# Moving half of the query/key projections and the value products in an attention block on one Trainium2 core

## The chip, the cores and the metric

The kernel runs on one core of a Trainium2 (trn2) chip. The metric is device time in microseconds (us). Before the change three runs took 684.49, 684.83 and 686.05 us, median 684.83.

## The reference

1024 tokens of width 512 go through two blocks. Both start with a layer norm over the 512 features and add their result to the residual stream. The second block is the one that the change touches. Cut to that:

```python
xn = layernorm(x)                                   # (1024, 512)
# attention, in the kernel's case one sequence of 1024 tokens, 32 heads of 16
q, k, v = xn @ Wq.T + bq, xn @ Wk.T + bk, xn @ Wv.T + bv
att = softmax(where(causal, q @ k.T / 4, -inf))     # per head
attn = (att @ v) @ Wo.T + bo
# feed-forward: a linear layer and 8 low-rank experts of rank 16
base = xn @ base_W.T + base_b
p = softmax(xn @ router_W.T + router_b)             # 15 routes, all of them kept
w = sum of p over the routes that map to an expert  # (1024, 8)
lora = ((xn @ A.T) * w) @ B.T * 2
x = x + attn + base + lora
```

The first block (a gated feed-forward of width 1248, a series of six terms and a top-2 low-rank mixture) is left as it is; it takes the first 250 us or so.

## The kernel before

**Arithmetic.** fp32 operands are split into a high and a low fp32r part. A product is then three matmuls, hi by hi, lo by hi and hi by lo (`product`, lines 894 to 896). ACT makes the high part and DVE the low part; for weights these are `split_hi` (line 696) and `split_lo` (line 1207), for projections `project_hi` (802) and `project_lo` (1413).

**Weights.** `weight_items` (line 75) lists 512 KB items in the order of use. SP loads them one after another into the two halves of `stage`, and ACT and DVE split each one to where it is used: two halves of `ring_hi`/`ring_lo`, or a place of its own. Item n is loaded once item n-2 is split. `ring_done` (468) says which projection frees a ring half.

**Queries and keys.** Each of the four 128-column parts m of the query and key projections serves two groups of four heads, groups 2m and 2m+1. A part is made by `project` (1004), 24 matmuls of 128x512 into one of two PSUM slots of two banks. ACT and DVE split it into `nat`, one set of SBUF tiles (a tile for q, one for k, each with a high and a low half), and SP stores both halves to `heads_dram` (`store`, 548). `project_hi` of part m waits until part m-1 has been stored (806), since all parts use the same tiles. `stack(g)` (523) loads group g from `heads_dram` in eight transfers, laid out so that a head's two query halves and one key half, with rows of ones, are the contraction rows. Four sets of stack tiles are used in turn: three of their own, and the last is what xt_hi and xt_lo leave free.

**Order on PE in the stage before attention.** After the first block's last transposes: q0 and the router, k0, q1, k1, q2, k2, q3, k3 (1035 to 1038), the rank-16 projection `a`, the gate transposes, eight value tiles (`values`, 1080) and eight tiles of the linear layer (`linear`, 1091). Between these stand the units of `maxima` (1048), 20 a group, which make a group's scores once to take each row's maximum; DVE reduces them in `row_max` (1451). Values carry the units of group 0, the linear layer those of group 1, and the attention steps those of groups 2 to 7, two groups ahead (`max_plan`, 228). `turn_maxima` (1074) transposes a group's finished maxima, `negate_max` (1467) negates them, `neg_max` (556) writes them into the query stack. The linear tiles end with the low-rank product from `hw1`, which lies in the ring half of item qk3 (466). `psum_users` (266) is the written-out order of everything that uses the two PSUM slots; the users take them alternately, and each waits for the one two places before it.

**Attention.** Eight groups of twelve steps (`QSTEPS`, 169). A step is a key tile against up to 512 queries of one half: widths 512, 384, 256, 128 in the first half, then 512, 384, 512, 256, 512, 128, 512, 512. Each step has four scores (`score`, 1123), one a head, in the order of heads 0, 2, 1, 3. At 512 or 384 columns each has a bank of its own, out of three used in turn. At 256 or 128 columns two heads share a bank (`score_bank`, 216): the first and third score fill one, the second and fourth the other, and ACT is told of a bank only when it is full. A score that opens a bank waits for the exponential of three banks before it. ACT takes the exponentials (872), POOL masks diagonal tiles (690), and `weigh_values` (1143) multiplies the probabilities of the step two before (LAG = 2) by the values into `bank[3]`: eight matmul records of 32 columns. `extras` (255) adds maxima units after the second and the fourth score, and in groups 6 and 7 parts of the output projection, three matmuls each, after the fourth. The value products stand last in a step (1183). Twice a group `take_u` (810) has ACT copy `bank[3]` out, ahead of the exponentials of steps 2 and 6, and the first value product of the next half waits for it (1151).

Issue order is the program's on every engine; PE, ACT, DVE, POOL and SP run on their own and wait on semaphores.

```python
1182                        k = STEPS * g + s - LAG
1183                        if hh == GH - 1 and k >= 0:
1184                            weigh_values(k)
```

Of the kernel before, what the change touches and what calls it, by code (L numbers as in the profile page):

```python
# [24 lines left out]
F32 = mybir.dt.float32  # L25
# [47 lines left out]
def weight_items():  # L73
# [192 lines left out]
def psum_users():  # L266
# [23 lines left out]
def build(nc, stream, router1, x_in, vec, bias_rows, discount, expert_map, heads_dram, den_dram, out):  # L290
    nodes = ExitStack()
    with nodes:
# [68 lines left out]
        u_sb = sb(block1, "u_sb", [P, 2, HALF])  # L361
        den = sb(block1, "den", [P, 2, DEN_COLS])
# [92 lines left out]
        for n, (dest, name) in enumerate(ITEMS):  # L455
            item_at[(name, sum(1 for d, m in ITEMS[:n] if m == name))] = n
            if dest == "ring":
                ring_at[n] = len(ring_at)
# [7 lines left out]
        hw1 = ring_of(f"qk{KD - 1}")[1:]  # L466
# [28 lines left out]
        def res(name):  # L495
# [6 lines left out]
        nat = {("q", 0): attn_hi[:, 2, :], ("q", 1): attn_lo[:, 2, :],  # L502
               ("k", 0): attn_hi[:, 3, :], ("k", 1): attn_lo[:, 3, :]}
# [4 lines left out]
        def _(sp):  # L508
# [11 lines left out]
            for n in range(2, item_at[("qk3", 0)] + 1):  # L520
                weights(n)

            def stack(g):
# [4 lines left out]
                if g < STACKS - 1:  # L528
                    sp.wait_ge(S["blank"], g + 1)
                if g == STACKS - 1:  # L530
                    sp.wait_ge(S["y_done"], NT)
# [16 lines left out]
            def store(which, m):  # L548

                sp.wait_ge(S[f"{which}_free"], m + 1)  # L550
                for part in range(2):
                    first = heads_dram[m, "qk".index(which), 0, part * HD]
                    sp.dma_start(bass.AP(first.tensor, first.offset, [[2 * HD * TOK, 2 * GH], [TOK, HD], [1, TOK]]),
                                 nat[which, part].bitcast(F32)).then_inc(S[f"{which}_stored"], 16)
# [61 lines left out]
            for g in range(GROUPS):  # L616
# [23 lines left out]
        def _(pool):  # L640
# [32 lines left out]
            for g in range(STACKS - 1):  # L673
# [4 lines left out]
            for t in range(NT):  # L678
                pool.tensor_tensor(x_sb[:, t, :], x_sb[:, t, :], bo_bc, ALU.add).then_inc(S["y_biased"], 1)
# [15 lines left out]
        def _(act):  # L695
            def split_hi(n):
# [6 lines left out]
                if dest == "base0":  # L703
                    act.wait_ge(S["q_stored"], 32 * KD)
                    act.wait_ge(S["k_stored"], 32 * KD)
                if dest == "wo0":
                    act.wait_ge(S["y_done"], NT)
# [92 lines left out]
            turned_hi(7)  # L800

            def project_hi(which, m):
# [4 lines left out]
                act.activation(nat[which, 0], slot_of((which, m))[:].rearrange("p a n -> p (a n)"), ACT.Identity,  # L807
# [10 lines left out]
            def attn_split_hi(m, half):  # L818
                k = 2 * m + half
                act.wait_ge(S["attn_f"], k + 1)  # L820
                if k == 0:
                    act.wait_ge(S["y_done"], NT)
                at = slice(half * HALF, (half + 1) * HALF)
# [7 lines left out]
            for m, names in enumerate((["qk2"], ["qk3"], ["lora1", "wv0"]), 1):  # L831
                for name in names:
                    split_hi(item_at[(name, 0)])
                project_hi("q", m)
                project_hi("k", m)
            split_hi(item_at[("wv1", 0)])
            act.wait_ge(S["a_ready"], 1)
            act.activation(lora_h1, slot_of(("a", 0))[:].rearrange("p a n -> p (a n)"), ACT.Copy
                           ).then_inc(S["a_free"], 1)
            act.wait_ge(S["w_free"], 1)  # L840
# [745 lines left out]
```

## Time and profile before

| what | us |
|---|---|
| median of three runs | 684.83 (684.49 to 686.05) |
| the profiled execution | 683.69 |
| its span, first to last instruction | 681.9 |
| PE busy in it | 613.8 (90%) |
| DVE / ACT / POOL busy | 377.8 / 293.3 / 77.0 |
| mean granted TensorE clock | 0.956 of full |

The profiled execution took 1.8 us more than its span, and 1.1 us less than the median. Times in rows are counted from the span's start. A row of the timeline gives start, duration, engine, line, operation, the tiles written and read, the shape, how many instructions it merges, and in square brackets the idle time of the engine ahead of it with what ended that. A matmul's duration contains its way through the array, so rows overlap: the time that PE needs for one is the distance between starts. A granted clock of 1.00 is 2.4 GHz, 0.50 is 1.2 GHz. The stages are: first block to 250 us, its tail and projections to 336, values to 373, linear layer to 416, attention to 662, tail to the end.

### The profile page before, as it was taken

The numbers are of one execution on the slowest core, as the hardware profiler recorded it, in microseconds if no ns is written. First come the engines' busy times: TensorE is split into PE (matmuls) and PEld (weight loads), VectorE is DVE, ScalarE is ACT, GpSimd is POOL, SyncE is SP. The second block draws the span as 40 slices with busy tenths as digits, with TensorE's granted clock in tenths as the row PEclk, the third lists the DMA queues.
The fourth block names the chain that finished last, engine by engine and source line by source line (L and its number), as shares of the span: only waits on it lengthen the run. The fifth ranks groups of instructions, "written<-read, shape, count | busy, mean of one in ns | idle before, by whom it ended". The sixth has DMA issues, their size and how long they took to land.

```text
span 681.9 us, 9359 instructions
## 1 busy us (share of the span) xinstructions
PE 613.8 (90%) x3688; PEld 404.4 (59%) x3688; DVE 377.8 (55%) x555; ACT 293.3 (43%) x509; POOL 77.0 (11%) x106
## 2 busy tenths in 40 slices
PE   2999999999999997974798987999999999998993
PEld 2788888878888874763566665434444444444441
DVE  5676553266543354622367457478898798822025
ACT  3456342133422222211321114577777677775540
POOL 3000000000000018100000222121211212121100
PEclk9999999999999997998799997599999899999996
DMA  6313313101111020469751001441633610100003
GB/s 218 123 63 124 122 64 124 62 32 62 43 52 62 32 79 15 125 206 178 266 181 32 3 1 31 75 95 36 111 75 65 108 30 18 26 20 17 21 18 135
DMA packets 24304, 53.64 MB, mean 79 GB/s; under 512 B 8880, under 2 KB 9392, under 8 KB 24256
## 3 DMA queue, kind: packets, MB, share of 16 engines
q1 hardware_dynamic: 23844, 52.33, 28.2%
q0 software_dynamic: 288, 0.58, 0.4%
q8 instruction: 29, 0.48, 0.3%
q10 hardware_dynamic: 128, 0.13, 0.1%
q14 instruction: 15, 0.12, 0.1%
HBM read 39.77 MB, written 10.61 MB: 74 GB/s over the span
## 4 chain that ended last, share of the span: by engine, by line
PE 75%; DVE 9%; DMA 7%; ACT 6%; issue 2%; SPq 1%; ACTq 0%; DVEq 0%
PE bank L1155 11%; PE bank L1138 10%; PE slot L894 8%; PE bank L894 7%; PE slot L896 7%; PE slot L895 7%; PE bank L896 7%; PE bank L895 7%; DMA heads_dram<-attn_lo 6%; PE slot L1061 5%; ACT probs L872 4%; PE slot L1069 2%; DVE maxcol L1460 2%; DMA stage<-in_stream 1%; PE slot L910 1%
## 5 line engine op out<-in xcount | busy, mean ns | idle before, releaser
L872 ACT ACTIVATE probs<-bank 128x512 f32<-128x512 f32 (+2 forms) x320 | 155.6, 560 | 71.4 <-PE bank L1138 69.6
L1460 DVE TENSOR_REDUCE maxcol<-slot 128x2 f32<-128x1024 f32 (+2 forms) x112 | 125.0, 1142 | 44.8 <-PE slot L1069 23.4
L894 PE MATMUL slot<-xt_hi,ring_hi 128*128 128x512 f32 (+2 forms) x248 | 99.7, 402 | 22.1 <-DVE attn_lo L1416 18.6
L895 PE MATMUL slot<-xt_lo,ring_hi 128*128 128x512 f32 (+2 forms) x248 | 98.4, 397 | 0.0
L896 PE MATMUL slot<-xt_hi,ring_lo 128*128 128x512 f32 (+2 forms) x248 | 98.2, 396 | 0.0
L1138 PE MATMUL bank<-qst,kst 50*128 50x512 f32 (+3 forms) x288 | 79.9, 444 | 6.8 <-ACT probs L872 5.9
L1155 PE MATMUL bank<-probs,v_sb 128*32 128x512 f32 (+3 forms) x768 | 85.4, 519 | 0.1
L1138 PEld LDWEIGHTS bank<-qst,kst 50*128 50x128 f32 x288 | 36.8, 199 | 68.2 <-ACT probs L872 59.4
L894 PEld LDWEIGHTS slot<-xt_hi,ring_hi 128*128 128x128 f32 (+2 forms) x248 | 47.4, 191 | 35.2 <-issue 22.0
L1061 PE MATMUL slot<-kst,qst 48*128 48x512 f32 (+3 forms) x288 | 58.3, 397 | 7.7 <-DVE maxcol L1460 7.6
L690 POOL TENSOR_SCALAR_AFFINE_SELECT probs<-probs 128x512 f32<-128x512 f32 x64 | 41.8, 653 | 200.9 <-ACT probs L872 200.9
L1460 DVE TENSOR_REDUCE maxrest<-slot 128x2 f32<-128x768 f32 (+3 forms) x48 | 49.7, 1044 | 21.3 <-PE slot L1069 21.1
L895 PEld LDWEIGHTS slot<-xt_lo,ring_hi 128*128 128x128 f32 (+2 forms) x248 | 47.6, 192 | 10.4
L896 PEld LDWEIGHTS slot<-xt_hi,ring_lo 128*128 128x128 f32 (+2 forms) x248 | 47.2, 190 | 10.7
L1371 DVE TENSOR_TENSOR h_f<-slot,silu 128x512 f32<-128x512 f32 (+1 forms) x20 | 13.8, 691 | 70.3 <-ACT silu L771 70.3
L771 ACT ACTIVATE silu<-slot 128x512 f32<-128x512 f32 (+1 forms) x20 | 12.0, 598 | 90.1 <-PE slot L896 90.0
L1061 PEld LDWEIGHTS slot<-kst,qst 48*128 48x128 f32 x288 | 31.2, 199 | 18.9 <-DVE maxcol L1460 11.5
L1069 PE MATMUL slot<-late_key,late_row 64*128 64x128 bf16 x512 | 35.8, 229 | 0.0
L1210 DVE TENSOR_TENSOR ring_lo<-stage,ring_hi 128x1024 fp32r<-128x1024 f32 x27 | 32.9, 1219 | 3.8 <-ACT ring_hi L708 3.8
L807 ACT ACTIVATE attn_hi<-slot,vec_sb 128x1024 fp32r<-128x1024 f32 x8 | 8.9, 1116 | 54.2 <-DMA heads_dram<-attn_lo 41.5
L1416 DVE SCALAR_TENSOR_TENSOR attn_lo<-slot,vec_sb,attn_hi 128x1024 fp32r<-128x1024 f32 x8 | 10.3, 1283 | 39.6 <-ACT attn_hi L807 39.6
L894 PE MATMUL bank<-res_hi,h_hi 128*128 128x512 f32 (+1 forms) x80 | 32.0, 400 | 0.2
(186 smaller groups left out, 880.8 us busy)
## 6 DMA issues: line engine op xcount, KB each, us to landing
stage<-in_stream SPq DMA_DIRECT2D x43, 512.0 KB, 3.5
heads_dram<-attn_hi SPq DMA_DIRECT2D x8, 512.0 KB
heads_dram<-attn_lo SPq DMA_DIRECT2D x8, 512.0 KB
qst<-heads_dram SPq DMA_DIRECT2D x12, 256.0 KB, 5.7
kst<-heads_dram SPq DMA_DIRECT2D x12, 256.0 KB, 9.7
stage<-u_sb SPq DMA_DIRECT2D x64, 32.0 KB, 2.0
out_y<-x_sb SPq DMA_DIRECT2D x8, 256.0 KB, 2.2
stage<-den_dram SPq DMA_DIRECT2D x15, 128.0 KB
```

Of the source, the lines that this page charges most:

```text
L690: pool.affine_select(out=part, in_=part, compare_op=ALU.is_ge, fill=0.0, base=0, pattern=[[0, GH], [1, P]], channel_multiplier=-1).then_in ...
L872: act.activation(probs[:, to:to + heads, 0:n], bank[b % 3][:, 0:heads * n].rearrange("p (h n) -> p h n", n=n), ACT.Exp, scale=HD ** -0.5). ...
L894: pe.matmul(out_ap, a[0], b[0], start=start, stop=False)
L895: pe.matmul(out_ap, a[0], b[1], start=False, stop=False)
L896: return pe.matmul(out_ap, a[1], b[0], start=False, stop=stop)
L1061: last = pe.matmul(ps[:, side, k * n:(k + 1) * n], queries(g)[rows, sl, i * P:(i + 1) * P], keys(g)[rows, sl, c:c + n], start=(k == 0), st ...
L1069: last = pe.matmul(ps[:, side, (k + 1) * n - P:(k + 1) * n], late_row[rows, part, :], late_key[rows, part, :], start=False, stop=(part == ...
L1138: last = pe.matmul(bank[b % 3][:, at * n:(at + 1) * n], keys(g)[rows, hh % 2, j * P:(j + 1) * P], queries(g)[rows, hh % 2, q0:q0 + n], sta ...
L1155: last = pe.matmul(bank[3][32 * hh:32 * hh + 2 * HD, c0:HALF], v_sb[:, j, (GH * g + hh) // 2, HD * (hh % 2):HD * (hh % 2 + 2)], probs[:, ( ...
L1210: dve.tensor_tensor(lo, stage[:, n % 2, :], hi.bitcast(F32), ALU.subtract).then_inc(S["w_lo"], 1)
L1371: dve.tensor_tensor(h_f[0:m, :], ps[0:m, 1, :], silu[0:m, :], ALU.mult).then_inc(S["h_f_ready"], 1)
L1460: dve.tensor_reduce(per_head[:, :, slots[0]:slots[-1] + 1], scores, AX.X, ALU.max).then_inc(S["max_free"], 1)
```

## The change

It does four things.

1. **Half of the projections go elsewhere.** Only q0, k0, q1 and k1 stand before `a`. q2 and k2 come between the values and the linear layer, q3 and k3 between the linear layer and attention, each pair with a `turn_maxima` between its two. The list of weights, SP's order, ACT's and DVE's orders and `psum_users` follow: the value weights are loaded and split before the projections, base0 and base1 are split after tiles 3 and 5 (ACT) and 4 and 6 (DVE) of the values, and SP loads stack 0 as soon as k0 is stored.
2. **Two sets of tiles.** `natural(which, m, part)` replaces `nat`: odd parts use the old tiles, even parts the third stack's tiles. `project_hi` of part m waits for the store of part m-2. Stack 2 gets its rows of ones by a transfer instead of a memset.
3. **`hw1` has tiles of its own**, 8 KB of each partition; the space reserved for POOL's transfer descriptors goes from 8192 to 2048 bytes of each partition. POOL adds the bias to residual tile t once value tile t is done.
4. **The value products move** from behind a step's fourth score to behind its second, and the extras of that place.

```diff
-    for m in range(KD):
-        add("ring", f"qk{m}")
-    add("ring", "lora1")
+    add("ring", "qk0")
+    add("ring", "qk1")
     for n in range(2):
         add(f"v{n}", f"wv{n}")
+    add("ring", "lora1")
+    add("ring", "qk2")
     for n in range(2):
         add(f"base{n}", f"base{n}")
+    add("ring", "qk3")
...
-    users += [("r", 0)] + [(which, m) for m in range(KD) for which in ("q", "k")]
+    users += [("r", 0)] + [(which, m) for m in range(2) for which in ("q", "k")]
     users += [("a", 0), ("w", 0)]
     for g in range(2):
-        users += [("max", UNITS * g + u) for u in range(UNITS)] + [("m", g)]
+        users += [("max", UNITS * g + u) for u in range(UNITS)] + [("q", 2 + g), ("m", g), ("k", 2 + g)]
...
+        hw1 = [sb(block1, f"hw1_{n}", [P, TOK], F32R) for n in ("hi", "lo")]
...
-        nat = {("q", 0): attn_hi[:, 2, :], ("q", 1): attn_lo[:, 2, :],
-               ("k", 0): attn_hi[:, 3, :], ("k", 1): attn_lo[:, 3, :]}
+        def natural(which, m, part):
+            if m % 2:
+                return (attn_hi, attn_lo)[part][:, 2 + "qk".index(which), :]
+            return (qst, kst)["qk".index(which)][:, 2, part, :]
...
-            for m, name in enumerate(("lora1", "wv0", "wv1", "base0")):
-                store("q", m)
-                store("k", m)
-                weights(item_at[(name, 0)])
-                if m in (1, 2):
-                    stack(m - 1)
+            store("q", 0)
+            store("k", 0)
+            stack(0)
+            store("q", 1)
+            weights(item_at[("base0", 0)])
+            store("k", 1)
             weights(item_at[("base1", 0)])
+            stack(1)
+            weights(item_at[("qk3", 0)])
+            weights(item_at[("wo0", 0)])
+            store("q", 2)
+            neg_max(0)
+            store("k", 2)
             stack(2)
-            for name in ("wo0", "wo1"):
-                weights(item_at[(name, 0)])
-            neg_max(0)
+            weights(item_at[("wo1", 0)])
+            store("q", 3)
             neg_max(1)
+            store("k", 3)
...
             for t in range(NT):
+                pool.wait_ge(S["v_done"], t + 1)
                 pool.tensor_tensor(x_sb[:, t, :], x_sb[:, t, :], bo_bc, ALU.add).then_inc(S["y_biased"], 1)
...
                 act.wait_ge(S[f"{which}_ready"], m + 1)
-                if m >= 1:
-                    act.wait_ge(S[f"{which}_stored"], 32 * m)
-                act.activation(nat[which, 0], ...
+                if m >= 2:
+                    act.wait_ge(S[f"{which}_stored"], 32 * (m - 1))
+                if m == 3:
+                    act.wait_ge(S["y_done"], NT)
+                act.activation(natural(which, m, 0), ...
...
-            project("k", 0)
-            for m in range(1, KD):
-                project("q", m)
-                project("k", m)
+            for m, which in ((0, "k"), (1, "q"), (1, "k")):
+                project(which, m)
...
             for t in range(NT):
                 values(t)
+            project("q", 2)
+            turn_maxima(0)
+            project("k", 2)
...
             for t in range(NT):
                 linear(t)
+            project("q", 3)
             turn_maxima(1)
+            project("k", 3)
...
-                        if hh == GH - 1 and k >= 0:
+                        if hh == 1 and k >= 0:
                             weigh_values(k)
...
+            project_lo("k", 0)
             for t in range(NT):
                 prod = hw_f1[:, t * NE * ROUTES:(t + 1) * NE * ROUTES].rearrange(
...
-                   dynamic_dma_scratch_size=8192)
+                   dynamic_dma_scratch_size=2048)
```

## Rows read from the trace of the kernel before

**Rows 1.** Waits, whole span: engine, line, what for; us, times, longest.

```profile
PE slot L894 <- DVE attn_lo L1416: 18.6, 5, 12.8
```

**Rows 2.** Timeline of PE, projections: first matmuls after waits, one projection, a slow restart.

```profile
296.42 0.47 PE L894 MATMUL slot<-xt_hi,ring_hi 128*128 128x512 f32 x1 [2.98 <-DVE attn_lo L1416]
...
302.71 0.47 PE L894 MATMUL slot<-xt_hi,ring_hi 128*128 128x512 f32 x1 [0.57 <-DVE attn_lo L1416]
...
308.01 0.39 PE L896 MATMUL slot<-xt_hi,ring_lo 128*128 128x512 f32 x1
...
328.56 0.76 PE L894 MATMUL slot<-xt_hi,ring_hi 128*128 128x512 f32 x1 [12.84 <-DVE attn_lo L1416]
...
332.11 0.46 PE L896 MATMUL slot<-xt_hi,ring_lo 128*128 128x512 f32 x1
```

**Rows 3.** Timeline of ACT and DVE: how a projection is split.

```profile
270.05 1.11 ACT L807 ACTIVATE attn_hi<-slot,vec_sb 128x1024 fp32r<-128x1024 f32 x1 [9.68 <-PE slot L896]
...
271.20 1.28 DVE L1416 SCALAR_TENSOR_TENSOR attn_lo<-slot,vec_sb,attn_hi 128x1024 fp32r<-128x1024 f32 x1 [2.77 <-ACT attn_hi L807]
```

**Rows 4.** Queue of SP, ACT's wait for a store, and a stack's transfers with their landing.

```profile
273.30 0.59 SPq L553 DMA_DIRECT2D heads_dram<-attn_lo  x1
...
282.81 1.12 ACT L807 ACTIVATE attn_hi<-slot,vec_sb 128x1024 fp32r<-128x1024 f32 x1 [4.41 <-DMA heads_dram<-attn_lo]
...
451.29 2.37 SPq L543 DMA_DIRECT2D qst<-heads_dram  x4
453.70 1.82 SPq L543 DMA_DIRECT2D kst<-heads_dram  x4
...
kst<-heads_dram SPq DMA_DIRECT2D x2, 256.0 KB, 7.0
```

**Rows 5.** Timeline of PE: the wait ahead of attention, and where group 1 starts.

```profile
418.30 0.39 PE L1077 MATMUL slot<-ident,maxcol 128*32 128x128 f32 x1 [2.06 <-DVE maxcol L1464]
...
451.85 0.50 PE L1138 MATMUL bank<-qst,kst 50*128 50x512 f32 x2
```

**Rows 6.** Windows: busy us of PE, PEld, DVE, ACT, POOL; clock, DMA share, GB/s.

```profile
418.00:442.00 24.00, 23.06 (x143) 12.80 (x147) 12.72 (x15) 14.00 (x28) 3.46 (x6) 0.51 0.41 73
...
534.00:562.00 28.00, 27.28 (x250) 12.53 (x250) 23.20 (x28) 20.63 (x43) 5.54 (x8) 0.94 0.43 78
```

**Rows 7.** Timeline of PE and ACT: a 512-column step of group 3 with maxima.

```profile
506.95 0.50 PE L1138 MATMUL bank<-xt_hi,xt_lo 50*128 50x512 f32 x2
...
507.29 0.35 PE L1061 MATMUL slot<-kst,qst 48*128 48x384 f32 x2
...
507.54 2.06 ACT L872 ACTIVATE probs<-bank 128x512 f32<-128x512 f32 x4 [0.26 <-PE bank L1138]
507.56 0.47 PE L1138 MATMUL bank<-xt_hi,xt_lo 50*128 50x512 f32 x1
...
508.19 0.49 PE L1138 MATMUL bank<-xt_hi,xt_lo 50*128 50x512 f32 x1 [0.16 <-ACT probs L872]
...
508.85 1.06 PE L1155 MATMUL bank<-probs,v_sb 128*32 128x512 f32 x8
...
509.84 0.44 PE L1138 MATMUL bank<-xt_hi,xt_lo 50*128 50x384 f32 x2
```

**Rows 8.** The same engines: step 2 of group 3, two heads a bank.

```profile
512.64 0.50 PE L1138 MATMUL bank<-xt_hi,xt_lo 50*128 50x256 f32 x4
...
512.77 0.60 ACT L816 ACTIVATE u_sb<-bank 128x512 f32<-128x512 f32 x1 [0.76 <-PE bank L1155]
513.27 1.08 ACT L872 ACTIVATE probs<-bank 128x512 f32<-128x512 f32 x2
```

**Rows 9.** Timeline of PE: a 512-column step of group 7 without extras.

```profile
626.24 0.73 PE L1138 MATMUL bank<-xt_hi,xt_lo 50*128 50x512 f32 x3
...
627.48 0.50 PE L1138 MATMUL bank<-xt_hi,xt_lo 50*128 50x512 f32 x1 [0.51 <-ACT probs L872]
...
628.91 0.61 PE L1138 MATMUL bank<-xt_hi,xt_lo 50*128 50x384 f32 x3
```

More of the change, by code:

```diff
@@ L519, in _ @@
             sp.dma_start(x_sb[:, 4:8, :], x_in[4:8].rearrange("t p d -> p t d")).then_inc(S["x_landed3"], 16)
-            for n in range(2, item_at[("qk3", 0)] + 1):
+            for n in range(2, item_at[("qk2", 0)] + 1):
                 weights(n)
@@ L527, in stack @@
                     sp.wait_ge(S["st_ready"], banks_before(g - STACKS + 1, 0))
-                if g < STACKS - 1:
+                if g < 2:
                     sp.wait_ge(S["blank"], g + 1)
+                if g == 2:
+                    for which in "qk":
+                        sp.wait_ge(S[f"{which}_stored"], 32 * 3)
                 if g == STACKS - 1:
-                    sp.wait_ge(S["y_done"], NT)
+                    sp.wait_ge(S["k_ready"], KD)
+                if 2 <= g < STACKS:
                     for side in range(2):
@@ L553, in store @@
                     sp.dma_start(bass.AP(first.tensor, first.offset, [[2 * HD * TOK, 2 * GH], [TOK, HD], [1, TOK]]),
-                                 nat[which, part].bitcast(F32)).then_inc(S[f"{which}_stored"], 16)
+                                 natural(which, m, part).bitcast(F32)).then_inc(S[f"{which}_stored"], 16)
             def neg_max(g):
@@ L672, in _ @@
             pool.wait_ge(S["xn_ready"], 2 * NT)
-            for g in range(STACKS - 1):
+            for g in range(2):
                 pool.memset(keys(g).rearrange("p b n -> p (b n)").bitcast(F32), 1.0).then_inc(S["blank"], 1)
@@ L800, in _ @@
             turned_hi(7)
+            for n in range(2):
+                split_hi(item_at[(f"wv{n}", 0)])
             def project_hi(which, m):
@@ L804, in project_hi @@
                 act.wait_ge(S[f"{which}_ready"], m + 1)
-                if m >= 1:
-                    act.wait_ge(S[f"{which}_stored"], 32 * m)
-                act.activation(nat[which, 0], slot_of((which, m))[:].rearrange("p a n -> p (a n)"), ACT.Identity,
+                if m >= 2:
+                    act.wait_ge(S[f"{which}_stored"], 32 * (m - 1))
+                if m == 3:
+                    act.wait_ge(S["y_done"], NT)
+                act.activation(natural(which, m, 0), slot_of((which, m))[:].rearrange("p a n -> p (a n)"), ACT.Identity,
                                bias=bias).then_inc(S[f"{which}_hi"], 1)
@@ L830, in _ @@
             project_hi("k", 0)
[L831 to L836, printed above, removed]
+            split_hi(item_at[("lora1", 0)])
+            project_hi("q", 1)
+            project_hi("k", 1)
             act.wait_ge(S["a_ready"], 1)
@@ L839, in _ @@
                            ).then_inc(S["a_free"], 1)
+            split_hi(item_at[("qk2", 0)])
             act.wait_ge(S["w_free"], 1)
-            act.wait_ge(S["k_ready"], KD)
-            act.activation(hw1[0], hw_f1, ACT.Copy).then_inc(S["hw_hi_ready"], 1)
+            act.activation(hw1[0][:], hw_f1, ACT.Copy).then_inc(S["hw_hi_ready"], 1)
             act.wait_ge(S["k_ones"], 1)
@@ L848, in _ @@
                                ).then_inc(S["v_free"], 1)
-                if t in (1, 3):
-                    split_hi(item_at[(f"base{t // 2}", 0)])
+                if t in (3, 5):
+                    split_hi(item_at[(f"base{t // 2 - 1}", 0)])
+            project_hi("q", 2)
+            project_hi("k", 2)
+            split_hi(item_at[("qk3", 0)])
             for t in range(NT):
@@ L1407, in _ @@
             turned_lo(7)
+            for n in range(2):
+                split_lo(item_at[(f"wv{n}", 0)])
             dve.wait_ge(S["const_ready"], 9)
@@ L1435, in _ @@
             spread(gate_x1, gate, NT)
-            project_lo("k", 0)
-            for m, names in enumerate((["qk2"], ["qk3"], ["lora1", "wv0"]), 1):
-                for name in names:
-                    split_lo(item_at[(name, 0)])
-                project_lo("q", m)
-                project_lo("k", m)
-            split_lo(item_at[("wv1", 0)])
+            split_lo(item_at[("lora1", 0)])
+            project_lo("q", 1)
+            project_lo("k", 1)
             dve.wait_ge(S["w_ready"], 1)
```

35 lines of the change are left out of this document (22 added, 13 removed).

## Prediction

> **What bounds the kernel.** I read the page first: PE busy 90%, and three quarters of the chain that ended last on PE, so only PE's waits and its clock are to be won or lost. The table of waits, PE alone, gives the stage before attention: PE waited 18.6 us in five places for DVE's low part of a projection, 12.8 in one [rows 1]. Its timeline shows them, and that the last began a restart at half clock: eight starts from 328.56 to 332.11 are 0.44 us apart against 0.23 before [rows 2]. DVE only follows ACT, and ACT waits until the previous part is stored: the second half of q0's store is issued at 273.30, ACT goes on at 282.81, 9.5 us later [rows 4]. So one set of tiles and the stores bound that stage. The next view is the wait ahead of attention, 2.06 us for the last maxima [rows 5], and the windows: from 418 to 442 the clock is 0.51 [rows 6]. Group 0 begins behind the transpose at 418.30, about 418.6, and ends at 451.85: 33.2 us; groups 1 and 2 take from there to 506.95, 27.6 each [rows 5, 7].
> In attention the thing to see is the loop between PE and ACT. A 512-column step starts at 506.95; ACT's first exponential starts 0.59 later; the fourth score waits for it and starts at 508.19; maxima, products at 508.85, next step at 509.84: 2.89 us [rows 7]. Without extras it is 2.67, with 0.51 idle [rows 9].
>
> **Projections apart, two sets.** A projection is 24 starts, 302.71 to 308.01, so 5.5 us [rows 2]. q0's end is marked by ACT's row at 270.05 [rows 3]; k0 starts about 270.6, and k0, q1, k1 and `a` end near 292.8, transposes 293.6, the first value tile (12 matmuls, 2.9) 296.5. None waits for a store: q1 and k1 have other tiles. DVE splits k0 before the gate products now. The waits [rows 1] (18.6) and the slow restart (8 x 0.21 = 1.7) [rows 2] go, and the wait for the last maxima (2.06) [rows 5] lies under q3: 22.4 us out.
> Late next is stack 0, which PE needs at 296.5. k0's split ends about 278.8, its store's second half is issued about 279.6, and with 9.5 it is stored at 289.1; a stack takes from 451.29 to one issue past 453.70 plus 7.0, about 10 us [rows 4]: 299, a wait of 2.5 (0 if nothing queues, 9 if transfers crowd).
> New waits stand where k2 and k3 take the slot that q2 and q3 just filled: `psum_users` leaves one short transpose between. ACT 1.11, DVE 1.28 and handovers are 2.6 [rows 3], less 0.3: 2.3 each. q2 waits some 0.6 for its slot. In: 2.5 + 0.6 + 4.6 = 7.7. Net -14.7.
> Each of the three waits over 2 us may bring half clock. The 2.98 us wait did not, the 2.06 with another ahead did [rows 2, 5]. Ends 0 and 3 x 1.7; I take one, 1.7: **-13.0**.
> The other moves I cost at nothing. The value weights' splits lie in DVE's and ACT's wait for the router. SP passes q1's and k1's stores, base0 and base1 behind stack 0, where nobody needs them for 12 us; stack 1, two ones rows in stack 2 and `neg_max(0)` have 30 us; if that cover went, each costs its 10 us. POOL's bias adds wait for values, read much later. POOL's six transfers keep their time if the smaller descriptor space holds them; if not, the first four wait for each other's landing, up to three landings of 7.0 [rows 4], 21 us at the start; they are few and small, so I leave that end out of the range. The page DMA: Bandwidth & Descriptors of the Trainium skill (SWDGE vs HWDGE) says those descriptors live in reserved SBUF rings; no row shows one full.
>
> **The clock at attention's start.** q3 and k3 are dense, but ACT owes k3's bias pass before the first exponential. Group 0's 33.2 us against 27.6 for the next two [rows 5, 7] bounds it: 0 to -5.6. Nearest is the 2.98 us wait with full clock, but two weight splits of ACT follow, so I take half: **-3**.
>
> **Products after the second score.** A full step now issues a pair of scores (506.95 to 507.29, 0.34), a maxima unit (to 507.56, 0.27), products with their wait (0.1 + 0.99), the second pair (0.34) and a unit with its diagonal (0.6): 2.64 against 2.89 [rows 7]. The wait for the step's first exponential is gone, since the products lie over it. Without extras the loop is 2.67 [rows 9] against 0.34 + 1.09 + 0.34 = 1.8, where ACT's four exponentials (2.06) become the bound.
> Against this stand two costs. (a) Steps of 256 and 128 columns, four of twelve, fill a bank only with the third score. Before, ACT could start after the four scores; now after the products too, up to 0.99 later. Step 7 (256 columns, no unit) shows it: pair 0.2, products about 0.9, pair 0.2, so the bank is full at 1.3, its exponential runs from 1.7 to 2.2, and the second score of step 8, which waits for it, starts at 2.3 where it could at 1.6 before: +0.7. Step 9 does the same to step 10, and step 3 to step 4. While PE multiplies, ACT has used up what was in the banks, so it starts late in the step after as well. (b) Step 2's products wait for `take_u`. Counted from step 1's start: pair 0.3, maxima 0.2, products 1.1, third score at 1.6, ACT from 2.15 with four of 0.41 to 3.8, copy 0.6, products 4.5, third score 5.5, step 2's exponentials from 5.8. Before, they started at 513.27, 3.4 after 509.84 [rows 7, 8]: 2.4 later, of which ACT's slack (0.76 idle before the copy alone [rows 8]) gives some back. Step 6 does this again, milder.
> Laid out so, with these durations, a group of maxima steps changes by: step 0 -0.2, steps 1 to 4 +2.0, 5 and 6 0, 7 to 9 (256, 512, 128) +1.9, 10 and 11 +0.4: +4.1. Groups 1 to 5: +20.5; group 0, whose first steps lack products, +1.9; group 6 -0.4; group 7, without maxima, gains 0.7 a full step against the cost of step 2: -3.5. **+18.5**. Ends: only the idle goes (8 x -0.25 in five groups, -5 in the last two: -15) and every cost in full (+6 a group: +35). I stay near the laid-out value, since it rests on rows 7 and 8.
> PE then idles more, and the clock already dipped in group 4 (0.94 over 28 us, about 1.7 us) [rows 6]. One more dip: **+2** (0 to the rival's).
>
> **Sum.** 683.7 (the profiled execution) - 13.0 - 3 + 18.5 + 2 = 688.2. It lay 1.1 below the median, so I predict 689.3; this case alone reaches 681 to 698. A measurement here tells 0.2%, 1.4 us, from no change.
>
> **Rivals.**
> *The products' move is free or gains.* ACT is idle a quarter of attention, and its late starts in narrow steps could be absorbed there; then only the removed idle counts. For it: the 0.51 us idle per step is in the rows [rows 9]. Against: three banks leave ACT no work while PE multiplies. Attention between -15 and +3, nearest -2: 683.7 + 1.1 - 13 - 3 - 2 = 667 (654 to 673). It decides at an attention cost under 14. Chance 0.23.
> *Half clock inside attention.* More idle per step brings the state of 418 to 442 [rows 6] back, at 5.6 us a group [rows 5]. With four groups: 689.3 + 22 = 711 (698 up). For: group 4's dip. Against: all other groups kept full clock. Chance 0.17. TensorE: Matmul & The Clock Gate of the Trainium skill (A second HAM failure mode) describes short idles between matmul groups, from cycling PSUM banks, as making the clock oscillate; by that rule this rival is the forecast, and group 4's dip agrees.
> *Stack 0 is late.* Stores and stack crowd, as they did when ACT waited longest; 6.5 more: 696. Chance 0.10.
> *The forecast* has 0.50.
>
> **Chances.** Faster: the first rival's 0.23 and 0.08 of the forecast's low end, 0.31. Same: 0.07. Slower: 0.62. The range, 664 to 704, holds the forecast, the third rival, most of the first and the start of the second.
>
> **What would show it.** Right: q1 to `a` without gaps over 0.6; values start near 294 and a PE wait for stack 0 of 1 to 4 us; two PE waits of 2.3 before k2 and k3; attention starting near 404; no wait of the fourth score; groups 1 to 5 of 31 to 33 us, with ACT idle over 1 us before steps 2, 3, 7 and 9, PE waiting at step 2's products for `u_sb`. Wrong: groups of 28 or less, or PE's clock at 0.5 for whole groups.

## The result, and the profile after

The changed kernel takes 707.88 us, median of four runs (700.97, 707.63, 708.12, 725.87), against 685.44 for the kernel before on the same chip: ratio 1.029, interval 1.0211 to 1.0368, so slower. The forecast was 689.3 with a range of 664 to 704: the sign was right, the size was not. Medians are over all runs, while ratios and intervals leave out, on both sides, the runs that are over about 1.5% longer than the fastest of the same kernel, so a ratio is not the quotient of the two medians. The profiled execution is the run of 700.97; its span is 699.2 at a mean clock of 0.954. The two middle runs had 0.937 and 0.942, the longest 0.904. The median is 6.9 us above the profiled execution, at a lower clock, and this trace does not show where that time lies.

In the changed kernel's numbering line 1163 is the scores (1138 before), 1180 the products with the values (1155), 896 the exponentials (872), 1083 the maxima (1061), 918 to 920 the three matmuls of a product (894 to 896), 1443 the low parts of the projections (1416), 835 the copy `take_u` makes of u (816).

The projections first. PE's waits from 280 to 420 (us in total, times, longest), which answer to [rows 1]:

```profile
PE slot L918 <- DVE qst L1443: 2.5, 1, 2.5
PE slot L918 <- DVE attn_lo L1443: 2.5, 1, 2.5
PE slot L918 <- DVE maxrest L1486: 0.6, 1, 0.6
```

and the timeline of PE there, which answers to [rows 2, 5]:

```profile
294.54 0.39 PE L920 MATMUL bank<-attn_hi,xt_lo 128*128 128x512 f32 x1
295.90 0.44 PE L1083 MATMUL slot<-kst,qst 48*128 48x128 f32 x4 [0.97 <-issue]
...
330.27 0.47 PE L918 MATMUL slot<-xt_hi,ring_hi 128*128 128x512 f32 x1 [0.59 <-DVE maxrest L1486]
...
333.94 0.45 PE L918 MATMUL slot<-xt_hi,ring_hi 128*128 128x512 f32 x1
...
340.19 0.47 PE L918 MATMUL slot<-xt_hi,ring_hi 128*128 128x512 f32 x1 [2.51 <-DVE qst L1443]
...
344.37 0.40 PE L920 MATMUL slot<-xt_hi,ring_lo 128*128 128x512 f32 x1
...
397.87 0.47 PE L918 MATMUL slot<-xt_hi,ring_hi 128*128 128x512 f32 x1 [2.50 <-DVE attn_lo L1443]
...
402.23 0.43 PE L918 MATMUL slot<-xt_hi,ring_hi 128*128 128x512 f32 x1
...
405.08 0.49 PE L1163 MATMUL bank<-qst,kst 50*128 50x512 f32 x2
```

The 12.8 us wait and its four companions are gone, the first value tile ends at 294.9, and attention starts at 405.08 instead of about 418.6: 13.5 us are won. What came in: 0.59 before q2, 2.51 before k2, 2.50 before k3, and a stretch at half clock behind each of the three. From 330.27 to 333.94 there are 9 steps from start to start, which at full clock take 2.04 (0.227 each): 1.6 lost. 340.19 to 344.37 loses 1.7 over 11 steps, 397.87 to 402.23 loses 1.6 over 12.

Then attention. The windows are groups 0, 3 and 6, then group 7 up to where the clock falls in the tail (busy us of PE, PEld, DVE, ACT, POOL; clock, DMA share, GB/s).

```profile
405.10:442.85 37.75, 35.07 (x226) 16.32 (x225) 20.00 (x19) 21.76 (x43) 4.46 (x7) 0.64 0.41 84
...
509.80:542.50 32.70, 29.05 (x266) 13.85 (x265) 23.92 (x27) 20.07 (x43) 5.10 (x8) 1.00 0.33 68
...
607.80:644.10 36.30, 33.71 (x203) 15.64 (x199) 11.18 (x17) 22.50 (x46) 5.64 (x9) 0.95 0.07 17
644.10:685.60 41.50, 36.94 (x209) 16.60 (x208) 9.45 (x15) 21.89 (x44) 5.41 (x9) 0.96 0.12 34
```

Here are the starts of the groups in both traces, and under each row of starts the lengths:

```
group              0      1      2      3      4      5      6      7+tail
before, start   418.62 451.85 479.72 506.95 535.14 563.59 591.80 626.24
before, length   33.2   27.9   27.2   28.2   28.5   28.2   34.4   55.7
after, start    405.08 442.85 477.30 509.78 542.54 575.02 607.79 644.10
after, length    37.8   34.5   32.5   32.8   32.5   32.8   36.3   55.1
```

Attention and tail grew from 263.3 to 294.1, by 30.8: +4.5 in group 0, +25.0 in groups 1 to 5, +1.9 in group 6, -0.6 after it. Groups 2 to 5 are at full clock, so their 32.6 against 27.7 (groups 2, 3 and 5 before, two even and odd neighbours averaged) is order, not clock: 4.9 a group. PE is busy 29.05 of 32.7 us where it was busy 27.28 of 28 [rows 6].

The page shows who waits. ACT has the same work as before and 104.5 us of idle ahead of its exponentials instead of 71.4, for scores; PE has a new wait, 4.2 in the row of the products. The first row is of the kernel before, the others of the changed one:

```profile
L872 ACT ACTIVATE probs<-bank 128x512 f32<-128x512 f32 (+2 forms) x320 | 155.6, 560 | 71.4 <-PE bank L1138 69.6
...
L896 ACT ACTIVATE probs<-bank 128x512 f32<-128x512 f32 (+2 forms) x320 | 155.2, 559 | 104.5 <-PE bank L1163 104.3
...
L1180 PE MATMUL bank<-probs,v_sb 128*32 128x512 f32 (+3 forms) x768 | 87.9, 531 | 4.8 <-ACT u_sb L835 4.2
```

**Step by step.** The products of one step follow those of the last, so the distance between their starts is a clean ruler for a step, even where a score's record is missing. Mean of two neighbouring groups at full clock (a group with and one without its `turn_maxima`); the column is the step into which the distance leads, widths 512, 384, 256, 128, 512, 384, 512, 256, 512, 128, 512, 512. E1 (below) has the projections of the changed kernel and the products of the kernel before; its distances are those of before.

```
step     0    1    2    3    4    5    6    7    8    9    10   11   sum
E1      2.26 2.62 1.88 1.36 3.00 2.59 2.30 1.66 2.93 1.36 2.47 3.26 27.7
after   2.42 2.85 2.98 2.39 3.01 2.93 2.34 2.72 3.04 2.43 2.34 3.20 32.6
E6      2.41 2.85 2.98 1.79 2.52 2.93 2.34 2.13 2.50 1.83 2.02 3.20 29.5
E9      2.41 2.85 2.98 1.36 2.38 2.94 3.39 1.66 2.15 1.83 2.02 3.20 29.2
E5      2.42 2.85 2.98 1.36 2.16 2.93 3.39 1.66 1.94 2.54 1.48 3.20 28.9
```

The loss stands in the four steps of 256 and 128 columns (2, 3, 7 and 9), 1.0 to 1.1 each, 4.3 of the 4.9. The full steps, where I had looked for a gain of 0.25 each, have mostly none. Step 7 of group 3 in the changed kernel, PE and then ACT:

```profile
528.43 0.50 PE L1163 MATMUL bank<-xt_hi,xt_lo 50*128 50x512 f32 x2
...
528.99 0.28 PE L1163 MATMUL bank<-xt_hi,xt_lo 50*128 50x256 f32 x1
529.61 0.38 PE L1163 MATMUL bank<-xt_hi,xt_lo 50*128 50x256 f32 x1 [0.34 <-ACT probs L896]
...
530.15 0.85 PE L1180 MATMUL bank<-probs,v_sb 128*32 128x384 f32 x8
530.93 0.62 PE L1163 MATMUL bank<-xt_hi,xt_lo 50*128 50x256 f32 x3
532.06 0.49 PE L1163 MATMUL bank<-xt_hi,xt_lo 50*128 50x512 f32 x1 [0.51 <-ACT probs L896]
```

```profile
528.96 1.09 ACT L896 ACTIVATE probs<-bank 128x512 f32<-128x512 f32 x2 [0.69 <-PE bank L1163]
531.41 2.07 ACT L896 ACTIVATE probs<-bank 128x512 f32<-128x512 f32 x4 [1.36 <-PE bank L1163]
534.71 1.08 ACT L896 ACTIVATE probs<-bank 128x512 f32<-128x512 f32 x2 [1.23 <-PE bank L1163]
```

Step 7 has four scores in two banks. The first two, 528.99 and 529.61, go into different banks, in the order 0, 2, 1, 3, so when the products begin at 530.15 neither is full. ACT finishes the last wide exponential at 530.05 and stands idle for 1.36 us; the third score, behind the products at 530.93, releases it at 531.41. Now PE waits: step 8's second score (532.06) had 0.51 to wait for ACT. In E1 the same step:

```profile
507.57 0.38 PE L1163 MATMUL bank<-xt_hi,xt_lo 50*128 50x256 f32 x2
...
508.02 0.28 PE L1163 MATMUL bank<-xt_hi,xt_lo 50*128 50x256 f32 x2
508.24 0.85 PE L1180 MATMUL bank<-probs,v_sb 128*32 128x384 f32 x8
```

```profile
508.40 3.28 ACT L896 ACTIVATE probs<-bank 128x512 f32<-128x512 f32 x6 [1.06 <-PE bank L1163]
```

All four scores are in the banks at 508.24, and ACT works through the products without a break, six exponentials in a row.

### The profile page after: what moved, and what is told of

Same layout as the page of the kernel before. It is cut to its first block, busy times and chain, and to the rows that moved or that the text cites. A ratio compares the mean times of both kernels' runs of the same rounds, so it can differ in the third digit from the quotient of the medians.

```text
span 699.2 us, 9361 instructions
## 1 busy us (share of the span) xinstructions
PE 631.2 (90%) x3688; PEld 413.8 (59%) x3688; DVE 378.2 (54%) x555; ACT 292.3 (42%) x509; POOL 76.2 (11%) x105
## 4 chain that ended last, share of the span: by engine, by line
PE 79%; DVE 8%; ACT 8%; issue 2%; DMA 1%; ACTq 0%; SPq 0%; DVEq 0%
PE bank L1180 11%; PE bank L1163 10%; PE slot L918 10%; PE slot L920 9%; PE slot L919 9%; PE bank L918 7%; PE bank L920 7%; PE bank L919 7%; ACT probs L896 5%; PE slot L1083 5%; DVE maxcol L1486 3%; PE slot L1091 2%; DMA stage<-in_stream 1%; PE slot L934 1%; DVE x_sb L1350 1%
## 5 line engine op out<-in xcount | busy, mean ns | idle before, releaser
L896 ACT ACTIVATE probs<-bank 128x512 f32<-128x512 f32 (+2 forms) x320 | 155.2, 559 | 104.5 <-PE bank L1163 104.3
L1163 PE MATMUL bank<-qst,kst 50*128 50x512 f32 (+3 forms) x288 | 90.2, 451 | 16.0 <-ACT probs L896 15.7
L1163 PEld LDWEIGHTS bank<-qst,kst 50*128 50x128 f32 x288 | 40.5, 197 | 87.9 <-ACT probs L896 58.9
L1180 PE MATMUL bank<-probs,v_sb 128*32 128x512 f32 (+3 forms) x768 | 87.9, 531 | 4.8 <-ACT u_sb L835 4.2
L1083 PE MATMUL slot<-kst,qst 48*128 48x512 f32 (+3 forms) x288 | 62.4, 398 | 9.5 <-DVE maxcol L1486 8.0
L1083 PEld LDWEIGHTS slot<-kst,qst 48*128 48x128 f32 x288 | 32.8, 197 | 19.4 <-DVE maxcol L1486 11.3
L1091 PE MATMUL slot<-late_key,late_row 64*128 64x128 bf16 x512 | 40.2, 227 | 0.0
L920 PE MATMUL bank<-res_hi,h_lo 128*128 128x512 f32 (+1 forms) x80 | 31.2, 390 | 0.0
L919 PE MATMUL bank<-res_lo,h_hi 128*128 128x512 f32 (+1 forms) x80 | 31.2, 390 | 0.0
```

What stands on the lines that cost most here:

```text
L896: act.activation(probs[:, to:to + heads, 0:n], bank[b % 3][:, 0:heads * n].rearrange("p (h n) -> p h n", n=n), ACT.Exp, scale=HD ** -0.5). ...
L919: pe.matmul(out_ap, a[0], b[1], start=False, stop=False)
L920: return pe.matmul(out_ap, a[1], b[0], start=False, stop=stop)
L1083: last = pe.matmul(ps[:, side, k * n:(k + 1) * n], queries(g)[rows, sl, i * P:(i + 1) * P], keys(g)[rows, sl, c:c + n], start=(k == 0), st ...
L1091: last = pe.matmul(ps[:, side, (k + 1) * n - P:(k + 1) * n], late_row[rows, part, :], late_key[rows, part, :], start=False, stop=(part == ...
L1163: last = pe.matmul(bank[b % 3][:, at * n:(at + 1) * n], keys(g)[rows, hh % 2, j * P:(j + 1) * P], queries(g)[rows, hh % 2, q0:q0 + n], sta ...
```

## The experiments

Each was run beside the kernel before on its chip: E1 to E4 and E5 to E8 in two sessions on one chip, E9 to E11 on another. The kernel before had medians of 688.4, 684.8 and 687.0 in these sessions, so between sessions the ratios are the safer comparison. "Group" is the mean of two neighbouring groups at full clock, as in the table.

**E1: the projections alone.**

```diff
-                        if hh == 1 and k >= 0:
+                        if hh == GH - 1 and k >= 0:
```

> The changed kernel with the value products back behind the fourth score. Theory P (the products' move costs about 5 us a group, the projections' move is worth about 13.5): attention starts near 405, groups 1 to 5 take 27.2 to 28.5 as before, the time is near 671, ratio 0.98. Rival C (most of the loss is half clock, set off by the new waits of 2.5 us before k2 and k3): groups 0 and 1 stay at 37 us, the time is 680 or more. Rival W (the new waits at the start of attention cost as such): group 0 stays near 37 at full clock.

Measured 669.25, ratio 0.9793 (0.9703 to 0.9883). Attention starts at 405.17, groups are 27.7 again, and group 0 takes 30.6 (33.2 before, 37.8 in the changed kernel), so neither rival holds. The projections' parts are a gain and the whole loss comes with the products.

**E2: the products alone,** the kernel before with `hh == 1`.

> The kernel before with the value products behind the second score, nothing else. Theory P: attention starts at 418.6 as before, groups 1 to 5 take 32.6 us, the time is 684.8 + 5 x 4.9 + 5 = 714, or more where the clock falls (ratio 1.04 or more). Rival C: groups take 28 to 29 at full clock and the time is under 695.

Measured 713.75, ratio 1.0401 (1.0265 to 1.0536); attention starts at 418.52 as before. The two parts multiply to 1.0401 x 0.9793 = 1.0186, against 1.029 (from 1.0211) for both; with E2's own interval of 1.3% either way they need no interaction. Its profiled execution was the longest of its runs (745.1), with half clock over most of 420 to 574, and groups 1 to 3 of 42 to 46. Group 4 is at full clock and takes 32.5, as groups 2 and 4 of the changed kernel do. Groups 6 and 7 are at full clock too:

```profile
655.10:731.20 76.10, 67.75 (x412) 30.92 (x409) 21.55 (x35) 44.79 (x91) 10.86 (x17) 1.00 0.11 33
```

From group 6 to the end E2 takes 88.3 us (655.1 to 743.4), the kernel before 90.1, the changed kernel 91.4.

**E3: early products in full steps only.**

```diff
+                        if hh == (1 if per_bank(s) == 1 else GH - 1) and k >= 0:
```

> The changed kernel with the products behind the second score only in steps of 512 and 384 columns; in the four narrow steps they are behind the fourth again. Theory P, cost a (a bank of a narrow step is full only with the third score): steps 7 to 9 fall from 8.0 to about 5.5 us and steps 1 to 4 from 10.7 to 8.5, groups of 28 to 28.5, time near 676. If the copy of the value sums (steps 2 and 6) is the main cost, step 6 keeps it and groups stay over 30.

Measured 668.59, ratio 0.9775 (0.9636 to 0.9914), group 29.0. The time came 7 us under the 676 expected, the group 0.5 over.

**E4: early products everywhere but in steps 2 and 6,** the two that wait for the copy of u: `hh == (GH - 1 if s in (LAG, HT + LAG) else 1)`.

> The changed kernel with the products behind the fourth score in steps 2 and 6 alone, where the first product waits for ACT's copy. Theory P, cost b: steps 1 to 4 fall by 1 to 1.5 us, step 6 hardly, steps 7 to 9 stay at 8.0; groups near 31, time near 697. If the copy is the main cost, groups fall under 29.5.

Measured 693.94, ratio 1.0124 (0.9995 to 1.0252). The narrow steps hold most of the loss: with them put back (E3) a group falls from 32.6 to 29.0, and the time is within its interval of E1's. In E4 a group with its transpose takes 31.9 against 33.1 in the changed kernel. That 1.2 is mostly step 3's distance, 1.25 against 2.39, because step 2 is narrow itself: putting its products back also fills its banks in time. So E4 did not isolate the copy.

**E5: as E3, and step 6 put back too.**

```diff
+                        if hh == (1 if per_bank(s) == 1 and s != HT + LAG else GH - 1) and k >= 0:
```

> The changed kernel with the products behind the second score only in steps of 512 and 384 columns other than step 6, so that both suspected costs are gone and only the gain of a full step is left. Theory P: groups 1 to 5 take 27 to 28 us, 0.3 to 1.5 less than with wide steps only; group 7 about 2 less than with the products last; time 665, between 662 and 668. If the gain of a full step is no gain in a group (PE's work bounds it anyway), the time is that of the projections' part alone, 669.

Measured 672.15, ratio 0.9842 (0.9765 to 0.992), group 28.9 (last row of the table) where 27 to 28 was expected. The gain isn't there: early products in full steps never bring one of groups 1 to 5 under E1's 27.7.

**E6: the narrow steps' banks full at the second score.** Everything early as in the changed kernel, but a step of 256 or 128 columns takes its heads in the order 0, 1, 2, 3.

```diff
-    hh = HEAD_ORDER[place]
-    return (place, 0) if per_bank(s) == 1 else (hh // 2, hh % 2)
+    return (place, 0) if per_bank(s) == 1 else (place // 2, place % 2)
...
-                hh = HEAD_ORDER[place]
+                hh = HEAD_ORDER[place] if per_bank(s) == 1 else place
```

> The changed kernel, products behind the second score everywhere, but in narrow steps the heads come in the order 0, 1, 2, 3, so that the first bank is full with the second score, ahead of the products. Theory P, cost a: steps 7 to 9 fall from 8.0 us to 6 to 6.5, groups from 32.6 to 30.5 or 31, step 2 keeps its wait for the copy; time near 697. If the late bank is not the cause, the groups stay at 32.6 or get longer, since two scores of one side can't overlap on PE.

**E7, its control:** E1 with the same order of heads.

> The same order of heads in the kernel with the projections' part alone, products last. Theory P: ACT is told of the first bank one pair sooner, and nothing waits for it there; within 1.5 us of the projections' part alone (669), either side. It is the control for the run before it.

E6 measured 682.31, ratio 0.9892 (0.9756 to 1.0029); E7 672.67, ratio 0.9881 (0.9777 to 0.9985), groups of 27.7. The order by itself leaves the group at E1's 27.7 (the median is 3.4 over E1's, outside the 1.5 expected, but the intervals of the ratios overlap). Under the early products it takes 3.1 us out of every full-clock group (32.6 to 29.5, better than the 30.5 expected) and 25.6 out of the median. Five groups of 3.1 are 15.5 of that; much of the rest stands beside a shorter half clock at attention's start, 407 to 414 in E6 against 409 to 436. Step 7 of group 4 of E6, PE and ACT:

```profile
538.19 0.85 PE L1179 MATMUL bank<-probs,v_sb 128*32 128x384 f32 x8
```

```profile
537.60 1.57 ACT L895 ACTIVATE probs<-bank 128x512 f32<-128x512 f32 x3 [0.69 <-PE bank L1162]
539.51 1.57 ACT L895 ACTIVATE probs<-bank 128x512 f32<-128x512 f32 x3 [0.33 <-PE bank L1162]
```

ACT takes the first narrow bank with its wide exponentials, under the products, and is idle 0.33 before the second bank, not 1.36. That is the mechanism shown by removing it. PE's waits over about four groups (us in total, times, longest: after, 477.3 to 607.8; E1, 464.1 to 575.6; E6, 462 to 581) say the same, and that the copy is still waited for:

```profile
PE bank L1163 <- ACT probs L896: 11.0, 34, 0.5
PE bank L1180 <- ACT u_sb L835: 2.3, 4, 0.6
```

```profile
PE bank L1163 <- ACT probs L896: 2.5, 11, 0.3
```

```profile
PE bank L1179 <- ACT u_sb L834: 4.4, 4, 1.3
PE bank L1162 <- ACT probs L895: 2.0, 8, 0.3
```

**E9: E6 with the products of steps 2 and 6 after the fourth score.**

> The changed kernel with the narrow steps' heads in bank order, so that a narrow step's first bank is full at its second score, and with the products of steps 2 and 6 after the fourth score again; all other products stay after the second. My theory, two separate costs: the narrow banks filled late are worth about 25 us (changed kernel against the bank-order run: 707.9 against 682.3) and the products waiting for the copy of u about 14 (707.9 against 693.9 with steps 2 and 6 put back). With both out the sum is 669, groups 1 to 5 take 27.5 to 28 us, and it stands within 5 us of the control with the products after the fourth score (672.7, groups of 27.3 to 28.2). The rival, that the place after the second score costs something of its own in every step (the matmul that now ends a step is a score, whose bank ScalarE waits for): groups of 29 or more, 680. A second rival, that it gains once its two costs are out: groups under 27, below 662.

Measured 683.16, ratio 0.9888 (0.9805 to 0.9971), group 29.2. My sum of two separate costs (669) fell, and the number is that of its first rival (680): putting the products of steps 2 and 6 behind the fourth score is worth 0.3 a group, and the distance into step 2 stays 2.98 wherever its products stand. The copy and the products of step 2 show why, first in group 3 of the changed kernel, then in group 3 of E9:

```profile
516.02 0.60 ACT L835 ACTIVATE u_sb<-bank 128x512 f32<-128x512 f32 x1
516.76 1.07 PE L1180 MATMUL bank<-probs,v_sb 128*32 128x512 f32 x8 [0.58 <-ACT u_sb L835]
```

```profile
503.01 0.61 ACT L834 ACTIVATE u_sb<-bank 128x512 f32<-128x512 f32 x1
503.76 1.06 PE L1179 MATMUL bank<-probs,v_sb 128*32 128x512 f32 x8
```

In both the products start 0.14 after the copy's end. Step 1's early products put off step 1's last exponentials, and the copy queues on ACT behind those, so at step 2 E9 did not take the copy's cost out (at step 6 it did: the products start 1.20 after its copy). A group of E9 is still 1.5 over 27.7; 1.1 of that is in the distance into step 2 and the other steps sum to 0.4, so the table doesn't show the rival's cost in every step either. No run has early products and the copy in time, so this 1.1 is read from rows and not shown by removing it.

**E10: the changed kernel with group 0 in the old order.**

```diff
+                        if hh == (GH - 1 if g == 0 else 1) and k >= 0:
```

> The changed kernel, but in group 0 alone the products come after the fourth score again. This asks whether the long half clock at the start of the attention (410 to 440 in the changed kernel, 410 to 415 where only the projections were moved) hangs on where group 0's products stand. If it does: full clock from about 415 to 425, group 0 near 31 us and group 1 near 32.6 (37.8 and 36.6 in the changed kernel), groups 2 to 5 still at 32.6, and a time of 694 to 698. If the half clock is a matter of how the PE comes into the attention, whatever the order in it: half clock to about 435 to 440 again, and 701 to 708.

Measured 707.35, ratio 1.0293 (1.0228 to 1.0358). The window from 410 to 430:

```profile
410.00:430.00 20.00, 20.00 (x119) 9.19 (x117) 10.39 (x10) 10.82 (x22) 3.22 (x5) 0.51 0.70 134
```

The rival holds: the half clock at the start of attention doesn't hang on the order of group 0 alone. It ends near 430 here, 6 us sooner than in the changed kernel, and group 0 takes 34.1 instead of 37.8; with one profiled execution of each, how much of that is the order stays open.

**E8: k2 and k3 straight behind q2 and q3,** in E1, since there each waited 2.5 us behind one short transpose.

```diff
-             [("q", 2 + g), ("m", g), ("k", 2 + g)]
+             [("q", 2 + g), ("k", 2 + g), ("m", g)]
...
             project("q", 3)
-            turn_maxima(1)
             project("k", 3)
+            turn_maxima(1)
```

The same for part 2, and DVE's `negate_max` and SP's `neg_max` go behind k as well.

> The projections' part alone, with k2 right behind q2 and k3 right behind q3 in the other slot and the transpose of the maxima after both. Theory P: the two waits of 2.5 us and their half-clock restarts (1.6 us each) go; at attention's start about 2 us come back as a wait of the first maxima unit for k3's slot. Attention starts near 398 and the time is 663 to 666. Rival: the first group then loses what was gained, and the time stays at 669.

Measured 660.52, ratio 0.9671 (0.9589 to 0.9753), the fastest of all here and 2.5 under what was expected. The end of the projections, PE:

```profile
395.03 0.50 PE L1163 MATMUL bank<-qst,kst 50*128 50x512 f32 x2
...
397.51 0.44 PE L1083 MATMUL slot<-kst,qst 48*128 48x128 f32 x4 [1.98 <-DVE attn_lo L1443]
```

Attention starts at 395.03, 10.1 before E1. The two waits (5.0) and the slow stretches behind them (3.3) are gone. The stretch behind q2's wait (1.6) didn't occur either, though E8 has that wait of 0.59 too, at 330.51; nothing in the edit explains it, so it may be luck. Behind attention's start 1.98 comes back as a wait of the first maxima for k3's slot.

**E11: E8 with the products after the third score** (`hh == GH - 2`), where the first narrow bank is full in the original order.

> The version with k2 and k3 next to q2 and q3 (660.5), with the products after the third score. A narrow step's first bank is full at its third score in this head order, so the late first bank is out of it; the second bank still waits for the products, and the products of steps 2 and 6 stand one score nearer to the copy of u. By my theory (first bank and copy are the costs) a group takes 28 to 29 us against 27.6, and the time is 661 to 668. The rival, that each score by which the products are moved forward costs the same (about half of the changed kernel's 4.9 us in a group): groups of 30, 677. If the place after the third score gains, because the fourth score's bank no longer waits: groups of 27 or less, 655.

Measured 667.08, ratio 0.9693 (0.9623 to 0.9763), group 28.4. As my theory had it, and no gain over E8: its interval overlaps E8's, and the full-clock group is 0.7 longer.

## Why the prediction was wrong

Most of the signs that it named came: two waits of 2.5 before k2 and k3, attention at 405, groups 1 to 5 of 32.6, ACT idle over 1 us at the narrow steps, PE waiting for `u_sb`. The steps of the sum that failed are the clock at attention's start, the gain of a full step, and the clock of the later groups and of the other runs. From 688.2 to the 701.0 of the profiled execution the parts are: projections -0.5, group 0 +5.6, groups 1 to 5 +4.5, groups 6 and 7 +1.8 without their half clock, half-clock dips +1.4. The median added 5.8 more.

**Projections, -13.0: right, -13.5,** though by parts that partly cancel. The waits before k2 and k3 were 2.5 each (forecast 2.3) and q2's 0.59 (0.6). Stack 0 cost at most 0.97 instead of 2.5: SP issued its q half at 281.06 and only the k half behind k0's store, where I had priced a whole stack:

```profile
281.06 3.94 SPq L551 DMA_DIRECT2D qst<-heads_dram  x4
288.23 1.71 SPq L551 DMA_DIRECT2D kst<-heads_dram  x4
```

The store was about as late as forecast (the k half could be issued at 288.23; 289.1 was forecast). q2's, k2's and k3's waits each had half clock behind them, 4.9 in all, where I had taken one stretch (1.7). 22.4 out, 6.6 and 4.9 in is 10.9. Of the other 2.6, 1.35 stands ahead of all PE work that was moved: q0 is done at 268.70 instead of 270.05 [rows 3].

```profile
268.70 1.12 ACT L826 ACTIVATE qst<-slot,vec_sb 128x1024 fp32r<-128x1024 f32 x1 [6.76 <-PE slot L920]
```

The last 1.2 is not traced. So that the total came within 0.5 is in part luck. The terms put at nothing cost nothing that shows: PE reaches q0's end no later than before, with POOL's smaller descriptor space too.

**The clock at attention's start, -3: wrong, and the first step that failed.** Group 0 came out at +4.5 over before, where this term and its share of the products (+1.9) made -1.1. The changed kernel is at half clock from 409.1 to 436.4, for 27.3 us, where the kernel before has 22.9 of it in group 0; half of the difference is 2.2, an estimate of what the clock cost instead of giving back 3. With the products last the term was near: E1's group 0 is 2.6 shorter than before. That isn't the order of the products (E10), and not the waits before k3 alone: E1, with the same projections, has one 5 us window at 0.50 (410 to 415) and one at 0.74, and E8 and E11, which have no such wait, differ as much from each other. Of E11:

```profile
396.60:437.60 41.00, 40.36 (x239) 20.41 (x237) 21.15 (x21) 22.98 (x45) 5.08 (x8) 0.50 0.43 103
```

while E8 is at half clock in 400 to 405 and at 0.82 over the next 15. What sets its length stays open; a forecast shouldn't book its end as a gain.

**Products, +18.5: mechanism right, size too small, and one part of it wrong.** At full clock a group costs 4.9 more, not 4.1, and groups 1 to 5 cost 25.0, not 20.5. Cost (a), the bank that only fills at the third score, I priced at 0.7 for steps 3, 7 and 9; it is 1.0 to 1.1 in each, and E6 takes 3.1 a group off. I had let ACT catch up in the step behind; steps 4, 8 and 10 gain at most 0.13. Cost (b), the copy, came much as laid out: counted from step 1's start (512.57 in group 3) step 2's products start after 4.2 (4.5 laid out) and its exponentials after 5.7 (5.8), 2.2 later than before, and 1.1 is left of that in the distance into step 2. It is the copy that is late, behind step 1's exponentials; where step 2's and 6's own products stand is worth 0.3 (E6 to E9). "The wait for the step's first exponential is gone" failed outright: it moved to the next step's second score. Behind a pair of full scores ACT has two exponentials, 1.0 us, to do under 1.0 us of products, and begins the next pair late. Hence no 0.25 a full step, and 0.2 to 0.3 lost in steps 1 and 5. In groups 6 and 7 with the tail, -0.4 and -3.5 stood and +1.9 and -0.6 came. But their clock is 0.95 and 0.96 in the windows above where it was 1.00 up to the tail before, an estimated 1.7 us each; without that it is -2.1, and E2, which has no half clock there up to the tail, is 1.8 shorter than before. So about half of this gain was real.

**More clock dips, +2: too little.** The profiled execution has one dip inside groups 1 to 5, 470 to 475, as before had one, and one each in groups 6 and 7, where before had none: 3.4 us. The other runs went from 707.6 to 725.9 as the mean clock went from 0.937 to 0.904, and the median sits 6.9 above the profiled execution, where I had added 1.1. So the half-clock rival, to which I had given a chance of 0.17, acts beside the forecast instead of in its place. The 0.2% that I said a measurement tells from no change was too narrow as well: beside E1 to E4 the kernel before alone ran from 678.2 to 697.3. The Trainium skill (TensorE: Matmul & The Clock Gate, A second HAM failure mode) says short idles from cycling PSUM banks make the clock oscillate. The traces agree in direction: between 450 and 565, half-clock stretches show in the profiled executions of the changed kernel, E2, E4 and E10, all with late narrow banks, also short in E11 and once before; E1, E3, E5, E6, E7, E8 and E9 have none. Against it: behind 565, in group 6, E1, E3, E7 and E8 have 7 to 14 us of half clock with the products last or with narrow steps put back, more than the changed kernel's 3.4 there. One profiled execution each isn't proof, and the cause of the dips stays open.

**The rivals.** The free move (667) fell with E5: even with the narrow steps and step 6 put back it gains nothing over E1, though the copy is late at step 2 there as well. Stack 0 late fell with 0.97. Half clock (711, from 698) was nearest to the median, though not by half clock in whole groups as it was priced: groups 2 to 5 of the profiled execution are at full clock, and the order alone makes most of the loss.

## What to carry over

Before moving work of one engine between two steps of another's input, mark what is handed over at the new place: a bank that two heads share is handed over when the second is in, and work put in front of that stalls the consumer for its full length. A wait for the consumer that is covered in one place can come back at the next point where the buffers run out; whether one more buffer would have helped was not tried. And a slot wait is cheapest hidden behind the neighbouring product: setting k behind q gave 10.1 us at attention's start and 8.7 in the median, 3.3 of them clock behind the two waits.

## What was not expected of the hardware

- PE's wait of 2.5 us before k2, between dense 128x512 matmuls, was followed by 3 to 4 us at half clock in eight of the nine profiled executions that have it (not in E7), and in most of them so was the 0.59 us before q2 (330.27 above); E8 has that wait at 330.51 without a slow stretch, and the 2.98 us before had none either [rows 2]. The stretch cost two thirds of the wait again.
- The half clock at the start of attention lasted from about 7 us (E8, E1, E6, E7; with 3 us more a little later in three of them) to 41 us (E11), there with PE busy 40.36 of 41.
- The same program on one chip spread from 675.8 to 714.6 (E9), its clock from 0.964 to 0.895; the kernel before, beside it, only from 678.8 to 689.7.
